# Moving the loads, sums and output weights of the first batch, and squaring the second weight group without GpSimd, in a fused Mamba-2 and feed-forward kernel

## What is computed

```python
xn = _layernorm(x)
# Mamba-2: zxbcdt = xn @ w_in; causal 4-tap convolution and silu on xBC; dt = softplus(dt + dt_bias)
# y = ssd(xh * dt, dt * A, B, C) + xh * D;  y = y * silu(z)
# y = y * rsqrt(mean(y * y) + EPS) * norm_w;  mamba = xn + y @ w_out
# feed-forward: hidden = fwht(silu(xn @ W1.T) * (xn @ W3.T));  ffn = hidden @ W2.T
out = x + mamba + ffn
```

## Time and profile before

| | us |
|---|---|
| median of 3 runs (lowest to highest) | 997.19 (996.74 to 998.36) |
| the profiled execution | 999.73 |
| its span | 997.9 |
| PE busy | 947.4 (95%) |
| DVE busy | 579.8 (58%) |
| ACT busy | 352.2 (35%) |
| POOL busy | 323.6 (32%) |

### The profile page before, as it was taken

The page is one execution under the profiler, slowest core; times in us unless marked ns, Lnnn a source line. Parts: engine busy times, 40 slices in busy tenths (PEclk is TensorE's granted clock), DMA queues, the critical chain, the costliest instruction groups (busy, mean ns, idle before and its releaser), DMA issues.

```text
span 997.9 us, 13278 instructions
## 1 busy us (share of the span) xinstructions
PE 947.4 (95%) x4999; PEld 473.0 (47%) x5000; DVE 579.8 (58%) x959; ACT 352.2 (35%) x544; POOL 323.6 (32%) x362
## 2 busy tenths in 40 slices
PE   8799858887999999999999999999999999999997
PEld 4344434443534444555545445554545445555543
DVE  7876567667453576655652576666551766665521
ACT  5587745423232333331221333332221344232200
POOL 2000524474200021863610202855510202855410
PEclk9999898888999999999999999999999999999999
DMA  9578452615431433544322434454322535255122
GB/s 335 198 239 305 168 160 73 211 45 177 137 106 64 172 102 109 179 139 120 113 85 64 162 105 137 138 159 118 115 64 64 172 105 153 73 156 148 43 75 94
DMA packets 76206, 134.25 MB, mean 135 GB/s; under 512 B 7536, under 2 KB 20464, under 8 KB 74096
## 3 DMA queue, kind: packets, MB, share of 16 engines
q1 hardware_dynamic: 56640, 104.88, 33.7%
q10 hardware_dynamic: 19504, 28.53, 9.2%
HBM read 107.43 MB, written 25.95 MB: 134 GB/s over the span
## 4 chain that ended last, share of the span: by engine, by line
PE 78%; DVE 9%; ACT 3%; POOL 3%; issue 3%; DMA 3%; ACTq 0%; DVEq 0%; SPq 0%; POOLq 0%
PE ps L594 51%; PE ps L831 15%; PE ps L792 2%; PE ps L784 2%; PE ps L778 2%; DMA arena<-cs_rows 2%; DVE arena L1227 2%; PE ps L718 1%; PE ps L747 1%; DVE arena L1173 1%; PE ps L764 1%; ACT arena L997 1%; POOL arena L1431 1%; ACT arena L917 1%; DMA arena<-w 1%
## 5 line engine op out<-in xcount | busy, mean ns | idle before, releaser
L594 PE MATMUL ps<-xh,arena 128*128 128x512 f16 x1592 | 492.7, 383 | 6.6 <-DVE arena L1173 6.6
L594 PE MATMUL ps<-xl,arena 128*128 128x512 f16 x796 | 304.7, 383 | 0.0
L594 PEld LDWEIGHTS ps<-xh,arena 128*128 128x128 f16 x1592 | 159.6, 100 | 196.9 <-issue 11.7
L831 PE MATMUL ps<-arena 128*128 128x512 f16 x768 | 171.1, 379 | 0.0
L1421 POOL TENSOR_TENSOR arena<-arena 128x512 f16<-128x512 f32 x64 | 78.7, 1234 | 237.5 <-ACT arena L967 237.5
L1431 POOL TENSOR_TENSOR arena<-arena 128x2048 f32<-128x2048 f32 x16 | 58.1, 3634 | 278.8 <-DMA arena<-cs_rows 278.8
L594 PEld LDWEIGHTS ps<-xl,arena 128*128 128x128 f16 x796 | 78.4, 99 | 90.3 <-issue 6.1
L831 PEld LDWEIGHTS ps<-arena 128*128 128x128 f16 x768 | 74.3, 98 | 91.0 <-issue 5.5
L1227 DVE SCALAR_TENSOR_TENSOR arena<-ps,cw,arena 128x511 f32<-128x511 f32 (+2 forms) x120 | 89.5, 748 | 45.6 <-ACT arena L957 43.7
L967 ACT ACTIVATE arena<-arena 128x512 f16<-128x512 f32 x64 | 40.3, 630 | 185.5 <-DVE arena L1248 185.5
L594 PE MATMUL ps<-wo_hi,arena 128*128 128x512 f16 x256 | 80.8, 388 | 0.2 <-DVE arena L1370 0.2
(11 more groups left out here) (182 smaller groups left out, 1094.3 us busy)
## 6 DMA issues: line engine op xcount, KB each, us to landing
arena<-w_parts SPq DMA_DIRECT2D x198, 256.0 KB, 2.7
w_parts<-arena SPq DMA_DIRECT2D x66, 256.0 KB, 3.0
arena<-cs_rows ACTq DMA_DIRECT2D x16, 1024.0 KB, 5.9
arena<-w SPq DMA_DIRECT2D x24, 512.0 KB, 4.8
...
```

The costliest lines, as they stand in the source:

```text
L594: ins = nc.tensor.matmul(out_ap, lhs(i, a), rhs(i, c), start=(i == 0 and s == 0), stop=(i == n - 1 and s == 2))
L831: ins = nc.tensor.matmul(bank(t), hw[a][:, i, t * P:(t + 1) * P], w2s[i % W2R][:, d, :], start=(i == 0 and s == 0), stop=(i == JF - 1 and ...
```

## The change

It has five parts.

1. Group 1's third piece is squared on ACT (the step G1S) instead of GpSimd. GpSimd's four squares, the four matmuls with bfloat16 ones and the cast that made those are gone; the sums of all pieces come from five columns of `row_sq`.
2. The raw loads of quads 5, 6 and 7 move, and quads 5 and 6 change buffers. Each quad has a QS of its own (eight instead of seven), and SQ and QS stand at other places.
3. WOQ q stands at place q + 2 of the A/U order, WOS moves from 9 to 11, the WOH by about two places.
4. A new step L issues the broadcast of the cumulative sums for chunks 1 to 3 (one DMA of ACT), two to seven tiles before the step E that uses it, in every batch. E keeps the two other loads.
5. N and Q of chunk 1, V, W and ROW move by one or two places; W of chunk 0 stands behind U8 instead of behind U7. The waits for bank 3 follow.

```diff
-QUAD_SUMS = ((0,), (1,), (2,), (3, 4), (5,), (6,), (7,))
-QUADS_EARLY = 4
-G1_ACT, G1_POOL, G1_DVE = 2, 2, 3
+QUADS_EARLY = 3
+G1_ACT, G1_DVE = 3, 3
-FIRST_AT = ([("WOL", 0, 1)] + [("WOQ", q, q // 2 + 4) for q in range(8)] + [("WOS", 0, 9)] +
+FIRST_AT = ([("WOL", 0, 1)] + [("WOQ", q, q + 2) for q in range(8)] + [("WOS", 0, 11)] +
...
-    for place, load in ((13, (4, 0)), (15, (4, 1)), (20, (6, 0)), (27, (5, 0)), (28, (5, 1)), (30, (6, 1)), (33, (7, 0)), (34, (7, 1))):
+    for place, load in ((13, (4, 0)), (15, (4, 1)), (20, (5, 0)), (28, (5, 1)), (30, (6, 0)), (32, (6, 1)), (35, (7, 0)), (36, (7, 1))):
...
+            if quad == 5:
+                return raw_pair if kind == 0 else hid_raw[:, :, 5]
             if quad == 6:
-                return raw_pair if kind == 0 else hid_raw[:, :, 7]
-            first = 5 if quad == 5 else 2 * quad
-            return hid_raw[:, kind, first:first + 2]
+                return hid_raw[:, :, 6 + kind]
+            return hid_raw[:, kind, 2 * quad:2 * quad + 2]
...
                         pe.wait_ge(sq_g1_dve, 1)
-                        pe.wait_ge(ones16_ok, 1)
-                        pe.wait_ge(sq_g1_pool, 4)
-                        for n in range(4):
-                            nc.tensor.matmul(bank(FREE_BANK), ones16, sq_pool[0][:, n * TILE:(n + 1) * TILE], start=(n == 0),
-                                             stop=False)
-                        pe_norm(pe, SQ_G1, SQ_G1 + 4, norm_sums, start=False)
+                        pe_norm(pe, SQ_G1, SQ_G1 + 5, norm_sums)
...
-                    elif kind == "E":
+                    elif kind == "L" or (kind == "E" and c == 0):
...
+                    elif kind == "E":
+                        act.wait_ge(d_cst, (b + 1) * 32)
+                        act.wait_ge(t1_ok.sem, t1_ok.at(b, c - 2))
+                        for r in range(2):
+                            act.dma_start(ecsb[HD * r:HD * r + HD, :].rearrange("p (q l) -> p q l", q=QE),
+                                          ecs_rows[b, c].rearrange("(q r) l -> r q l", r=2)[r].partition_broadcast(HD)).then_inc(d_ecsb, 16)
...
-            nc.vector.tensor_copy(ones16, ones).then_inc(ones16_ok, 1)
...
-                        to_scale(IN1, bank(FREE_BANK), ALU.add)
+                        to_scale(IN1, bank(FREE_BANK)[:, 0:5], ALU.add)
...
-            pool.wait_ge(d_g1[G1_POOL], 16)
-            for n, tile in enumerate(range(*G1_PIECES[G1_POOL])):
-                w = staged[:, tile - 2, :]
-                nc.gpsimd.tensor_tensor(sq_pool[0][:, n * TILE:(n + 1) * TILE], w, w, ALU.mult).then_inc(sq_g1_pool, 1)
```

More of the change, by code:

```diff
@@ L319, in build @@
         sq_act = [at(a, CHUNK // 2).bitcast(BF16) for a in (xr_at, acc_at)]
-        sq_pool = [at(a, CHUNK // 2).bitcast(BF16) for a in (hs_at, racc_at + CHUNK // 2)]
+        sq_dve = at(racc_at + CHUNK // 2, CHUNK // 2).bitcast(BF16)
         w2_raw = at(csbc_at, JF * D)
@@ L371, in build @@
         d_xr = [sem(f"d_xr{i}") for i in range(2)]
-        sq_g0, sq_g1, sq_g1_pool, sq_g1_dve, sq_wo = (
-            sem(n) for n in ("sq_g0", "sq_g1", "sq_g1_pool", "sq_g1_dve", "sq_wo"))
+        sq_g0, sq_g1, sq_g1_dve, sq_wo = (
+            sem(n) for n in ("sq_g0", "sq_g1", "sq_g1_dve", "sq_wo"))
         sq_w2 = sem("sq_w2")
@@ L634, in pe_cumsums, with pe_norm @@
             ins.then_inc(pe_cst.sem, 1)
-        def pe_norm(pe, lo, hi, done, start=True):
-            nc.tensor.matmul(bank(FREE_BANK)[:, 0:hi - lo], ones, row_sq[:, lo:hi], start=start, stop=True).then_inc(done, 1)
+        def pe_norm(pe, lo, hi, done):
+            nc.tensor.matmul(bank(FREE_BANK)[:, 0:hi - lo], ones, row_sq[:, lo:hi], start=True, stop=True).then_inc(done, 1)
         @block.tensor
@@ L727, in _ @@
                             pe.wait_ge(sq_w2_dve, JF // 4)
-                        elif i in (4, 6):
-                            pe.wait_ge(yscl_ok.sem, yscl_ok.at(0, (i - 4) // 2))
                         elif i == 5:
-                            pe.wait_ge(mamba_evac.sem, mamba_evac.at(0, 0))
-                        pe.wait_ge(sq_quads, 2 * (QUAD_SUMS[i][-1] + 1))
-                        lo, n = QUAD_SUMS[i][0], len(QUAD_SUMS[i])
+                            pe.wait_ge(yscl_ok.sem, yscl_ok.at(0, 0))
+                        elif i == 6:
+                            pe.wait_ge(mean_read.sem, mean_read.at(0, 0))
+                        elif i == 7:
+                            pe.wait_ge(yscl_ok.sem, yscl_ok.at(0, 1))
+                        pe.wait_ge(sq_quads, 2 * (i + 1))
                         to = bank(FREE_BANK)
-                        nc.tensor.matmul(to[:, 2:2 + 2 * n], ones, row_sq[:, SQ_Q + 2 * lo:SQ_Q + 2 * (lo + n)], start=True, stop=False)
-                        ins = nc.tensor.matmul(to[:, 2:2 + 2 * n], ones, row_sq[:, SQ_FREE:SQ_FREE + 2 * n], start=False, stop=True)
+                        nc.tensor.matmul(to[:, 2:4], ones, row_sq[:, SQ_Q + 2 * i:SQ_Q + 2 * i + 2], start=True, stop=False)
+                        ins = nc.tensor.matmul(to[:, 2:4], ones, row_sq[:, SQ_FREE:SQ_FREE + 2], start=False, stop=True)
                         if i == 3:
@@ L926, in _ @@
             nc.scalar.activation(nega[:], nega[:], ACT.Exp).then_inc(alog_e, 1)
-            for k in range(1):
+            for k in range(2):
                 act.wait_ge(d_g1[k], 16)
@@ L1145, in to_scale @@
             def to_scale(n, sums, op):
-                k = steps.step(nc.vector.tensor_reduce(out=total[:, n:n + 1], in_=sums, axis=AX.X, op=op))
+                v, h = total[:, n:n + 1], half[:, n:n + 1]
+                k = steps.step(nc.vector.tensor_reduce(out=v, in_=sums, axis=AX.X, op=op))
                 dve.wait_ge(steps.sem, k)
-                scale_of(n, 1, total[:, n:n + 1])
-            def scale_of(n, m, v):
-                h = half[:, n:n + m]
                 k = steps.step(nc.vector.tensor_scalar(h.bitcast(I32), v.bitcast(I32), 1, 0x3F800000, ALU.logical_shift_right,
@@ L1155, in scale_of @@
                 dve.wait_ge(steps.sem, k)
-                steps.step(nc.vector.tensor_scalar(scl[:, n:n + m].bitcast(I32), h.bitcast(I32), -1, 204 << 23, ALU.mult, ALU.add))
-                k = steps.step(nc.vector.tensor_scalar(inv[:, n:n + m].bitcast(I32), h.bitcast(I32), 1, 50 << 23, ALU.mult, ALU.add))
+                steps.step(nc.vector.tensor_scalar(scl[:, n:n + 1].bitcast(I32), h.bitcast(I32), -1, 204 << 23, ALU.mult, ALU.add))
+                k = steps.step(nc.vector.tensor_scalar(inv[:, n:n + 1].bitcast(I32), h.bitcast(I32), 1, 50 << 23, ALU.mult, ALU.add))
                 dve.wait_ge(steps.sem, k)
```

53 lines of the change are left out of this document (21 added, 32 removed), and 6 rows, old and new, of the table FIRST_AT.

## The result

| | before | changed |
|---|---|---|
| median, us (runs) | 997.78 (4) | 1003.53 (4) |
| lowest to highest | 996.74 to 998.92 | 1003.33 to 1006.06 |
| span of the profiled execution | 997.9 | 1004.2 |

The ratio is 1.0063, with a 95% interval of 1.0043 to 1.0084: the changed kernel is slower by 4 to 8 us. I had forecast 990.7, with 985.0 to 999.5 as the range. Both forecast and range are wrong, and so is the sign.

What follows compares the result with a forecast made beforehand. Batch 0's schedule, where nearly all TensorE gaps lie, was taken as the bound. Terms -2.0 - 1.8 - 2.2 - 0.5 = -6.5 us gave 993.2 profiled; the runs' median lies 2.5 lower, hence 990.7, range 985 to 999.5.

Steps and rivals of the forecast that it cites:

- part 5: Clock behind H0 in batch 0, -2.2 us; batches 1 to 3, GpSimd's wait going in part, -0.5 (-0.7 to +1.5).
- Part 1: Batch 0, second group's squares: scale ready at 25.7 instead of 27.7, everything behind shifts by -2.0 us.
- Part 2: Batch 0, ACT meets WOQ0 early and waits 6.2 us for w_out: U1's high copy +4.2 us, debt then shrinking.
- Part 3: Batch 0, WOS0 behind QS4: A5's split meets E1's subtraction, WOS0 runs 11 us after A5, QS5 +3.6 us.
- rival A: Batch 0, no collision of A5's split with GpSimd's subtraction: WOS0 and N0 3.5 us earlier, 987.2 us; chance 0.15.
- Part 4: Batch 0, W0 behind U8 and waits removed: U8 evicted 0.5 us earlier, H0 1.8 us earlier than before.
- rival C: Batch 0, QS6 waits for SQ6 and the clock falls over W0's matmuls: +5.0 us, 1002 us; chance 0.20.
- the term of -1.8: End of the gains in batch 0: H0 runs 1.8 us earlier than in the kernel before.

Runs made afterwards that it cites:

- part 1 alone: Kernel before with only group 1's third piece squared on ACT, GpSimd's four squares and their matmuls gone: 996.98 us, ratio 0.9978.
- the old kernels with part 1: Kernel before with group 1's third piece squared on ACT (0.9978), and that plus early load and held GpSimd subtraction in batches 1 to 3 (0.9947).
- The experiments on the stalls: Changed kernel, GpSimd's subtraction held behind DVE in batches 1 to 3, plus batch 0 holds (chunks 1, 3: 0.9938; all: 0.9921), later QS5/QS6 (0.9953), or chunks 1, 3 and QS (0.9934).
- the changed kernel with the late load: Changed kernel with L put back beside E (places 6, 14, 22) in batches 1 to 3, batch 0 as changed: 996.35 us, ratio 0.9967.

## Why the prediction was wrong, step by step

The step that failed is the last sentence of part 5: "GpSimd's earlier E may block DVE, but TensorE has no gap there to grow; between -0.7 and +1.5". It gave -0.5 for batches 1 to 3 and they gave +10.1. "No gap" was read as "slack", and these are two things. The mean of a slice says that TensorE waits for nothing there now; how late a partner may come before it does wait is the time from the partner's end to TensorE's use. The rows at 433 to 438 us of before give it. GpSimd's low part ends at 434.12, so without its wait for the load it would subtract from there, 0.6 us before DVE's Y instruction at 434.76. In the earlier trace rows a split that starts inside the subtraction ends 0.55 us behind it (100.23 + 3.12 against 99.19 + 3.61), its own 0.75 less 0.2. So DVE would end at 434.12 + 3.61 + 1.29 - 0.2 = 438.8 instead of 436.05, 2.8 late. The slack to N's matmul is 438.58 - 437.24 = 1.3. So 1.4 us of wait, twice a batch: measured 1.26 to 1.27. I had used this very mechanism for batch 0, with the rule of the Trainium skill beside it, and didn't carry it to the loop that runs three times.

The other steps, by the rows of the changed kernel's timeline:

```profile
26.15 0.72 ACT L911 ACTIVATE arena<-arena,scl 128x512 f16<-128x512 f32 x1 [1.65 <-DVEq L1261]
...
104.02 0.72 ACT L1016 ACTIVATE arena<-arena,nw 128x512 bf16<-128x512 f32 x1 [6.05 <-DMA arena<-w_out]
...
137.40 3.63 DVE L1165 SCALAR_TENSOR_TENSOR arena<-arena,scl 128x512 f16<-128x512 f32 x1 [2.32 <-ACT arena L911]
...
142.37 0.60 PE L637 MATMUL ps<-row_sq,con 128*128 128x9 f32 x2 [10.99 <-DVE f L1275]
...
155.61 0.56 PE L730 MATMUL ps<-row_sq,con 128*128 128x2 f32 x2 [3.54 <-issue]
...
176.55 0.56 PE L730 MATMUL ps<-row_sq,con 128*128 128x2 f32 x2 [3.37 <-ACT arena L991]
...
186.24 0.68 DVE L1239 SCALAR_TENSOR_TENSOR arena<-ps,arena 128x512 f32<-128x512 f32 x1
...
244.22 1.10 PE L742 MATMUL ps<-arena,hads 128*128 128x512 f32 x2
```

- *Part 1, -2.0.* The split behind group 1's scale stood at 26.15 against 27.79: 1.6 us in this execution, 2.2 (0 to 4) by the timed ratio of part 1 alone. Right, as far as the interval can tell.
- *Part 2, the load of w_out.* ACT's wait forecast at 6.2, measured 6.05; U1's high copy forecast at 108.8 (110.8 less the front's 2.0), measured 108.82. Right.
- *Part 3, the new stall.* A collision of A5's split with E1's subtraction, 3.63 us instead of 0.75; WOS0 forecast 11 us after A5, at 142.6, measured 10.99 and 142.37; QS5 forecast at 155.6, measured 155.61. Right to a few tenths, and rival A falls. One reading was wrong: that the trace of before had only GpSimd first. The rows at 194.60 and 194.88 above have DVE first, and there DVE took its 0.75 us and GpSimd 3.94 instead of 3.61.
- *Part 4, the gains up to H0.* This is the second step that failed, by its sizes. U8's eviction forecast at 184.1 (0.5 + 2.0 earlier than the 186.6 of before), measured 186.24. The mechanism of rival C came: TensorE waited 3.37 us for SQ6, and the clock fell behind it:

```profile
177.00:183.00 6.00, 6.00 (x42) 4.54 (x43) 5.05 (x11) 1.81 (x4) 4.74 (x14) 0.57 0.22 45
```

  I had given it nothing; the 2.1 us by which U8's eviction missed are some measure of it, not the 7 of rival C. H0 came at 244.22, not at 241.8, and beside the old kernels with part 1 (241.72 and 242.12) it wasn't earlier at all: the term of -1.8 has nothing to stand on. The experiments on the stalls show why such terms can't be added: an earlier H0 had its 3.7 us taken back by the clock behind it.
- *Part 5, the clock behind H0, -2.2.* The changed kernel took 77.63 us from H0 to H15 and the kernel before 80.08: 2.4 less. It holds in every profiled execution (77.6 against 79.4 to 80.1), and for the reason forecast. Right.

Of the sum of -6.5, -6.0 were to stand at the end of batch 0. The profiled execution showed -3.8 there: -1.4 up to H0 instead of -3.8, and -2.4 behind it. The timed ratio of the changed kernel with the late load, which has all of batch 0's change, says -3.3 (-4.7 to -2.0). Then came +10.1. The last sentence of the prediction named the case ("All fails if GpSimd's earlier E opens gaps in batches 1 to 3"), with no chance and no price. Six waits of 1.4 us are 8.4, and in place of the -0.5 they turn the sum of -6.5 into +2.4.
